# Sixteen-head attention: row maxima passed on per eight heads, and turned scores 17 heads behind the straight ones

## The reference

```python
qkv = x @ in_proj_weight.T + in_proj_bias            # x is the normed input
q, k, v = ...                                        # (B, 16 heads, 256, 8) each
bias = jnp.minimum((pos[:, None] - pos[None, :]) * slopes[:, None, None], MAX_BIAS)
scores = q @ k^T * 8 ** (-0.5) + bias
probs = jax.nn.softmax(scores, axis=-1)
out = (probs @ v) @ out_proj_weight.T + out_proj_bias
```

## Time and profile before

| | us |
|---|---|
| median of 3 runs | 1011.14 (1010.91 to 1011.57) |
| the profiled execution, its own time | 1014.49 |
| its span on the core | 1012.5 |
| mean granted TensorE clock, share of full speed | 0.899 |
| TensorE busy (matmuls) | 795.3 |
| VectorE busy | 550.0 |
| ScalarE busy | 400.2 |
| GpSimd busy | 358.3 |

### The profile page before, as it was taken

One profiled execution on the slowest core, in us unless ns is written; L12 is line 12 of the kernel. 1 busy time (PEld: TensorE's weight loads), 2 busy tenths in 40 slices (PEclk: granted clock), 3 DMA queues, 4 the chain that ended last, 5 costly groups with the idle time before them and its releaser, 6 DMA issues.

```text
span 1012.5 us, 19075 instructions
## 1 busy us (share of the span) xinstructions
PE 795.3 (79%) x5669; PEld 573.7 (57%) x5669; DVE 550.0 (54%) x2190; ACT 400.2 (40%) x945; POOL 358.3 (35%) x543
## 2 busy tenths in 40 slices
PE   0788488999999999932688989889899983029894
PEld 0677365655665777722255666666666652018784
DVE  4677573233222333232777889887897725016772
ACT  0466121222212332200055667665667672015562
POOL 4000517777850232343123323232232011744552
PEclk9999658999999999976579999998999996559998
DMA  9960001111100133114544354433444005111110
GB/s 247 155 207 0 1 1 35 39 42 40 40 0 14 56 110 109 58 52 100 116 93 90 77 106 92 85 86 68 105 90 81 3 3 187 51 56 52 52 50 14
DMA packets 75114, 72.44 MB, mean 72 GB/s; under 512 B 8125, under 2 KB 65680, under 8 KB 72732
## 3 DMA queue, kind: packets, MB, share of 16 engines
q1 hardware_dynamic: 69436, 60.38, 26.6%
q0 software_dynamic: 5600, 11.12, 3.4%
HBM read 43.71 MB, written 27.33 MB: 70 GB/s over the span
## 4 chain that ended last, share of the span: by engine, by line
PE 50%; DVE 14%; issue 10%; DMA 10%; POOL 6%; SPq 4%; ACT 3%; DVEq 2%; POOLq 0%; ACTq 0%
PE bank L1468 10%; PE bank L1469 9%; PE bank L1491 6%; DMA arena<-back_rows 5%; DVE rt L1066 4%; PE bank L1520 4%; POOL sorted_rows L766 3%; PE bank L1610 2%; PE bank L1562 2%; PE bank L1597 2%; PE bank L1592 2%; SPq L527 2%; DMA qk_parts<-arena 2%; SPq L548 1%; PE bank L1411 1%
## 5 line engine op out<-in xcount | busy, mean ns | idle before, releaser
L1066 DVE CUSTOM_DVE_ANT_0 rt<-bank,alibi 128x256 f32<-128x256 f32 x512 | 192.8, 419 | 43.7 <-PE bank L1562 36.6
L1276 ACT ACTIVATE arena<-bank 128x512 f32<-128x512 f32 x256 | 150.6, 597 | 75.7 <-PE bank L1597 69.8
L974 DVE TENSOR_TENSOR arena<-arena,bank 128x512 f32<-128x512 f32 (+1 forms) x128 | 75.1, 587 | 188.6 <-ACT arena L1249 188.6
L1249 ACT ACTIVATE arena<-bank 128x512 f32<-128x512 f32 (+1 forms) x128 | 66.1, 517 | 203.9 <-PE bank L1469 203.9
L1562 PE MATMUL bank<-arena 72*128 72x256 bf16 x512 | 105.9, 292 | 41.0 <-DVE arena L1066 27.1
L1592 PE MATMUL bank<-arena 81*128 81x256 bf16 x512 | 119.3, 279 | 6.5 <-ACT arena L1276 4.6
L1468 PE MATMUL bank<-arena 128*128 128x320 f32 (+2 forms) x256 | 117.2, 540 | 7.3 <-DVE arena L974 7.3
L1469 PE MATMUL bank<-arena 128*128 128x320 f32 (+2 forms) x256 | 112.5, 521 | 0.0
L1562 PEld LDWEIGHTS bank<-arena 72*128 72x128 bf16 x512 | 38.8, 103 | 86.1 <-DVE arena L1066 57.4
L1597 PE MATMUL bank<-arena,ident_b 128*128 128x256 bf16 (+8 forms) x544 | 83.8, 250 | 0.0
L1469 PEld LDWEIGHTS bank<-arena 128*128 128x128 f32 x256 | 49.7, 194 | 43.1 <-issue 32.8
(11 more groups left out here) (236 smaller groups left out, 1378.9 us busy)
## 6 DMA issues: line engine op xcount, KB each, us to landing
arena<-qk_parts SPq DMA_DIRECT2D x48, 192.0 KB
arena<-qk_parts SPq DMA_DIRECT2D x144, 64.0 KB
qk_parts<-arena SPq DMA_DIRECT2D x16, 384.0 KB, 2.8
back_rows<-empty_row SPq DMA_DIRECT2D x1, 4096.0 KB, 38.5
arena<-back_rows SPq DMA_DIRECT2D x16, 256.0 KB, 8.8
arena<-in_w SPq DMA_DIRECT2D x2, 2048.0 KB, 10.9
xg_rows<-empty_row SPq DMA_DIRECT2D x1, 2580.0 KB, 38.5
arena<-xg_rows SPq DMA_DIRECT2D x8, 322.5 KB, 4.0
```

Source lines behind the costliest of these rows:

```text
L974: nc.vector.tensor_tensor(out, sil[:, k, 0:out.shape[1]], bank[4 + k][:, 0:out.shape[1]], ALU.mult).then_inc(hid_done, 1)
L1066: last = nc.vector.tensor_tensor_reduce(biased[n % 2 * QT + u], bank[n % 2][:, SEQ * u:SEQ * u + SEQ], alibi[:, h, P * (1 - u):P * (1 - u) ...
L1249: nc.scalar.activation(sil[:, k, 0:width], bank[2 + k][:, 0:width], ACT.Silu).then_inc(sil_done, 1)
L1276: nc.scalar.activation(prT3[:, n % (2 * HG)].rearrange("p k t -> p (k t)"), bank[2 + n % 2][:], ACT.Exp).then_inc(exp3_done, 1)
```

## The change

- The maxima are handled per half batch m = 0 to 31 of MH = 8 heads: the split at 8m + 9 and 8m + 10, the turning at 8m + 12, the copy at 8m + 13. `max_part` and `max_rest` are half as wide.
- ScalarE issues the DMA of the maxima itself: `copy_max(m)` waits until its own copy is done and issues a DMA of 24 rows into `qs`. `send_max` leaves SP's program. `score_turned` waits for a half's DMA at its first head.
- EXP_LAG goes from 25 to 17, and with it BACK from 45 to 37.
- The steps of the norm move: `combine` from -41 and -40 to -43 and -41, the statistics from -39 to -36, the variance from -38 to -34, `norm3` from -33 to -32. The projection and the copy of q and k stay.
- TURN_5 to LOGITS_5 come two slots earlier behind BACK. ROOT_LAG goes from 5 to 4, so that GpSimd does `root5(c - 4)` behind `parts(c)`.
- The waits on the shared PSUM bank and on the maxima are rewritten for halves.

```diff
-EXP_LAG = 25
-COMBINE_0, COMBINE_1, STATS, VARIANCE, NORM, TURN, HT, QKV, QK_COPY, VALUES = -41, -40, -39, -38, -33, -30, -29, -26, -25, -19
-SPLIT_MAX_0, SPLIT_MAX_1, TURN_MAX, COPY_MAX = NH + 1, NH + 2, NH + 4, NH + 5
+EXP_LAG = 17
+MH = NH // 2
+COMBINE_0, COMBINE_1, STATS, VARIANCE, NORM, TURN, HT, QKV, QK_COPY, VALUES = -43, -41, -36, -34, -32, -30, -29, -26, -25, -19
+SPLIT_MAX_0, SPLIT_MAX_1, TURN_MAX, COPY_MAX = MH + 1, MH + 2, MH + 4, MH + 5
...
-NORM_5, TURN_5, COPY_5, ROUTER_5, LOGITS_5 = BACK + 22, BACK + 27, BACK + 28, BACK + 30, BACK + 31
-ROOT_LAG = 5
+NORM_5, TURN_5, COPY_5, ROUTER_5, LOGITS_5 = BACK + 22, BACK + 25, BACK + 26, BACK + 28, BACK + 29
+ROOT_LAG = 4
...
+def half_batch_at(slot, offset):
+    m, r = divmod(slot - offset, MH)
+    return m if r == 0 and 0 <= m < 2 * BATCH else None
...
-        def send_max(c):
-            wait_apart(sp, (max_rows_done, c + 1))
-            sp.dma_start(qs[MROW:KALL, c % RING], max_rows[0:PARTS * NH, c % 2]).then_inc(max_in[c % 2], 16)
...
-            send_max(c)
...
-        def copy_max(c):
-            act.wait_ge(max_tr, c + 1)
-            if c >= 2:
-                act.wait_ge(max_in[c % 2], 16 * (c // 2))
-            nc.scalar.activation(max_rows[0:PARTS * NH, c % 2], bank[7][0:PARTS * NH, 0:P].bitcast(BF16), ACT.Copy).then_inc(max_rows_done, 1)
+        def copy_max(m):
+            act.wait_ge(max_tr, m + 1)
+            if m >= 2:
+                act.wait_ge(max_in[m % 2], 16 * (m // 2))
+            nc.scalar.activation(max_rows[0:PARTS * MH, m % 2], bank[7][0:PARTS * MH, 0:P].bitcast(BF16), ACT.Copy).then_inc(max_rows_done, 1)
+            c, h = m // 2, MH * (m % 2)
+            wait_apart(act, (max_rows_done, m + 1))
+            act.dma_start(qs[MROW:KALL, c % RING, h:h + MH], max_rows[0:PARTS * MH, m % 2]).then_inc(max_in[m % 2], 16)
...
-            if h == 0:
-                pe.wait_ge(max_in[c % 2], 16 * (c // 2 + 1))
+            if h % MH == 0:
+                m = n // MH
+                pe.wait_ge(max_in[m % 2], 16 * (m // 2 + 1))
```

More of the change, by code:

```diff
@@ L267, in _build @@
     nmax3 = carve([P, 2, QT, NH])
-    max_rest = carve([P, QT, NH])
-    max_part = carve([P, QT, PARTS, NH], BF16)
+    max_rest = carve([P, QT, MH])
+    max_part = carve([P, QT, PARTS, MH], BF16)
     max_rows = carve([P, 2, SEQ], BF16)
@@ L1061, in row_max @@
             wait_apart(dve, (s3_mm, n + 1), *([(max3_done, n - 1)] if n >= 2 else []))
-            if h == 0 and c >= 2:
-                dve.wait_ge(max_parts_done, c - 1)
+            if h % MH == 0 and c >= 2:
+                dve.wait_ge(max_parts_done, n // MH - 3)
             for u in range(QT):
@@ L1069, in row_max, with max_parts_0, max_parts_1 @@
             last.then_inc(max3_done, 1)
-        def max_parts_0(c):
-            wait_apart(dve, (max3_done, NH * (c + 1)), *([(max_tr, c)] if c >= 1 else []))
-            nm = nmax3[:, c % 2]
+        def max_parts_0(m):
+            wait_apart(dve, (max3_done, MH * (m + 1)), *([(max_tr, m)] if m >= 1 else []))
+            nm = nmax3[:, m // 2 % 2, :, MH * (m % 2):MH * (m % 2) + MH]
             nc.vector.tensor_copy(max_part[:, :, 0, :], nm).then_inc(max_split, 1)
-            dve.wait_ge(max_split, 3 * c + 1)
+            dve.wait_ge(max_split, 3 * m + 1)
             nc.vector.tensor_tensor(max_rest, nm, max_part[:, :, 0, :], ALU.subtract).then_inc(max_split, 1)
-        def max_parts_1(c):
-            dve.wait_ge(max_split, 3 * c + 2)
+        def max_parts_1(m):
+            dve.wait_ge(max_split, 3 * m + 2)
             nc.vector.tensor_copy(max_part[:, :, 1, :], max_rest).then_inc(max_split, 1)
-            dve.wait_ge(max_split, 3 * c + 3)
+            dve.wait_ge(max_split, 3 * m + 3)
             nc.vector.tensor_tensor(max_part[:, :, 2, :], max_rest, max_part[:, :, 1, :], ALU.subtract).then_inc(max_parts_done, 1)
@@ L1118, in _ @@
                 row_max(n)
[L1119 to L1122, removed]
+            if (m := half_batch_at(slot3, SPLIT_MAX_0)) is not None:
+                max_parts_0(m)
+            if (m := half_batch_at(slot3, SPLIT_MAX_1)) is not None:
+                max_parts_1(m)
             if (c := batch_at(slot3, COMBINE_0)) is not None:
@@ L1341, in _ @@
                 copy_qk(c)
-            if (c := batch_at(slot3, COPY_MAX)) is not None:
-                copy_max(c)
+            if (m := half_batch_at(slot3, COPY_MAX)) is not None:
+                copy_max(m)
             if (c := batch_at(slot3, COPY_OUT)) is not None:
@@ L1544, in project @@
             if c >= 3:
-                pe.wait_ge(max_rows_done, c - 2)
+                pe.wait_ge(max_rows_done, 2 * c - 4)
             for a in range(2):
@@ L1564, in score, with turn_max @@
             last.then_inc(s3_mm, 1)
[L1566 to L1572, removed]
+        def turn_max(m):
+            pe.wait_ge(max_parts_done, m + 1)
+            if m >= 1:
+                pe.wait_ge(max_rows_done, m)
+            pe.wait_ge(qk3_done, min(m // 2 + 3, BATCH))
+            if m >= 7 and m % 2 == 1:
+                pe.wait_ge(lg5_done, (m - 5) // 2)
             for u in range(QT):
-                last = nc.tensor.transpose(bank[7][0:PARTS * NH, P // 2 * u:P // 2 * u + P // 2].bitcast(BF16),
+                last = nc.tensor.transpose(bank[7][0:PARTS * MH, P // 2 * u:P // 2 * u + P // 2].bitcast(BF16),
                                            max_part[:, u].rearrange("p a h -> p (a h)"), ident_b[:])
@@ L1638, in turn5 @@
             pe.wait_ge(h5_done, e + 1)
-            pe.wait_ge(qk3_done, min(e + 7, BATCH))
-            pe.wait_ge(max_rows_done, min(e + 4, BATCH))
+            pe.wait_ge(qk3_done, min(e + 6, BATCH))
+            pe.wait_ge(max_rows_done, min(2 * e + 7, 2 * BATCH))
             if e >= 1:
@@ L1668, in _ @@
                 project(c)
-            if (c := batch_at(slot3, TURN_MAX)) is not None:
-                turn_max(c)
+            if (m := half_batch_at(slot3, TURN_MAX)) is not None:
+                turn_max(m)
             if (c := batch_at(slot3, TURN_0)) is not None:
```

## The result

The changed kernel takes 1077.4 us (median of 4 runs, 1074.4 to 1080.3) against 1011.0: 6.6% slower, ratio 1.066 (95% interval 1.063 to 1.069). The forecast was 1068, within 1042 to 1100.

A forecast was written before the change was run, and what follows sets the result against it. It took a 41.7 us loop over two batches as the bound, TensorE close behind. Terms -7.5 + 57.2 + 3 + 2.4 + 2 = +57.1 on the profiled 1014.5 gave 1071.6, as a median 1068 us; range 1042 to 1100.

The forecast's parts named there:

- The bound before: Stage of the kernel before: a loop spanning two batches, 41.7 us long, sets the pace, with TensorE close behind.
- the loop of two batches: Copy of q and k, parts, replicate, given-row load, combine, next copy: 41.7 us before, +2.4 us with the change.
- The loop of one batch: Given rows, combine, variance, root5, parts, replicate, next given rows: 27.4 us per batch, +57.2 over nine turns, combines 6 to 15.
- The signs named: Combines 27 us apart, VectorE's given-row wait some 50 us or more, split right behind root5, TensorE idle some 7 us a turn.
- Up to combine 6: Start of the stage: two more slots from combine 4 to the next copies, TensorE slow: +3 us (0 to +6).
- the step on the maxima: Extra VectorE, TensorE and ScalarE work and DMA issues for half batches, covered by TensorE's 8 us idle per turn: 0.
- Behind combine 15: Combine 15 two slots later, +2.4 us; TensorE restarting after an idle stretch, +2 (0 to +5).
- the tail of turned scores: End of the stage: eight slots with turned scores alone go, at 0.94 us each: -7.5 us.
- up to 2.5 us per batch: Cost of the extra small operations and DMA issues for the maxima if no TensorE idle time covered them.
- 8 in all: TensorE's wait per turn if the maxima's DMA landed late: some 4 us twice a batch, equal to its idle time.
- The rival of the cold clock: TensorE drops to 1.2 GHz after idling each turn; if it stays low longer, turns of 31 us, 1100 us; chance 0.09.
- The rival by which the loop of two batches remains: Variance ready in time, so root5 costs parts nothing: +8.7 us, 1020 us; chance 0.12.

The follow-up runs named there:

- Experiment 5: Kernel before the change, with the load of given rows issued ahead of the replicate reads on SP: 995.9 us, ratio 0.982 to the kernel before.
- experiment 7: Kernel before the change, with only the norm's offsets moved as in the change: ratio 1.014 to the kernel before.
- 3: Changed kernel with residual_variance two slots later (BACK + 21 instead of BACK + 19): ratio 1.108 to the kernel before.
- experiment 4: Changed kernel with the load of given rows issued ahead of the replicate reads on SP: ratio 1.001 to the kernel before.
- experiment 1: Changed kernel with residual_variance four slots earlier (BACK + 15 instead of BACK + 19): ratio 1.060 to the kernel before.
- experiment 2: Changed kernel with ROOT_LAG back at 5 instead of 4: ratio 1.116 to the kernel before.
- experiment 8: Changed kernel with the norm's offsets and ROOT_LAG 5 as before, leaving halves, ScalarE's DMA and the lag of 17: ratio 1.137 to the kernel before.

## Why the prediction was right

**The bound before.** Right. Experiment 5 removes the loop of two batches and gains 1.8%, experiment 7 lengthens it by two slots and loses 1.4%.

**The loop of one batch.** Right in place and size: 27.2 us per turn against 27.4, nine turns 244.5 against 246.6. Its two parts fit as well: from the combine to SP's write of the parts 10.0 us against 10.5, from there to the combine it frees 17.2 against 16.9, so a small part of the agreement is two misses that cancel. Each station stands in the chain quoted above; a shift within the loop moves the time (3), and taking the load out of it takes the loss away (4). The signs named came too: VectorE's wait for given rows of 61.4 us, the split right behind `root5`, TensorE idle 5.7 us a turn (I had said some 7).

**Up to combine 6.** The term that was mis-sized: +3 forecast (0 to +6), +11.3 measured. What failed is the step on the maxima, "so 0": it counted ScalarE's DMA as hidden by 8 us of idle time in a turn, and that time exists only once the loop runs, from parts(5) on. Ahead of it a half's DMA met the twelve reads, TensorE waited 5.6 us and came back slow, and the stretch from combine 4 to 5 was 9.2 us longer. The figure of 9.2 us that I gave for a transfer behind a replicate was the right one for this DMA.

**Behind combine 15.** Forecast +2.4 + 2 - 7.5 = -3.1, measured -3.1. The equality is luck: up to the last row maximum it was +3.1 where I had 4.4 (now 881.6 - 809.92, before 812.2 - 743.59), and the tail of turned scores gave -6.2 where I had -7.5 (now 898.8 - 881.6, before 23.4).

**Sum.** Forecast +57.1, measured +64.2 between the profiled spans and +66.3 between the medians. The miss is the first part's.

**What the forecast did not see** is how much it depended on its own idle time. It said what the waits of ScalarE and TensorE would cost without that cover, "up to 2.5 us per batch" and "8 in all", and experiments 1, 2 and 8 gave 6 to 13 us per turn above experiment 4. Over nine turns these are 55, 83 and 116 us more, of which TensorE's busy time, longer by the slow level, is 20, 25 and 70; the rest is idle time, and only in experiment 8 is the clock the larger part. Experiment 1, meant as a cure, failed because a cost that had been covered came out; experiment 2 failed by a step that I had missed, the root ahead of root5. The rival of the cold clock came true in small: each of the nine turns has a clock of 0.87 to 0.94, and the loss fits in TensorE's idle time, as computed. The cause of the changed kernel's time is the load behind the split; the remedy was not to shorten the way to the split but to take the load out from behind it. The rival by which the loop of two batches remains, 1020 us, was never seen by itself: experiment 1, which takes `root5`'s wait out of the way, has the late DMAs of maxima on top.

## What to carry to other kernels

In a pipeline with programs written out per engine, follow each wait back through the queues that it stands in until it closes on itself, and divide the length by the number of batches that it spans. If that is more than the busiest engine's work per batch, it is the turn (27.2 us here, with 19.3 of work on TensorE); if not, the engine is (19.7 with 19.0 of work in experiment 5). A load whose data are ready early doesn't belong behind transfers that wait for late ones; moving one DMA issue was worth 1.8% in the kernel before and 6% in the changed one. And a cost put at nothing because idle time hides it must be priced again before that idle time is taken away.

## What the runs showed of the hardware

- A DMA that ScalarE issues doesn't pass reads that SP has issued. In the changed kernel the 24 packets of 512 bytes of a half's DMA issued at 542.09, with no reads in flight, start 1.4 us after the issue, and it lands after 2.0. In the case above the first of them starts 7.0 us after the issue and the DMA lands after 9.2; up to its first packet only packets of SP's queue run, of 8192 and 1024 bytes. In experiment 1, right behind the reads, it lands after up to 11.3. This is no sooner than the load of given rows in SP's own queue, mostly 8 to 11 us. By the Trainium skill ("DMA: Bandwidth & Descriptors", Queues, rings and completion order) each DMA engine alternates between the rings of different issuers; if it did so between these two, the small DMA should have been done early in the drain. The measurement decides: a separate queue gave no precedence here. The same page says (Issuing engines are not separate DMA queues) that issuing from several engines saves issue time only, and these runs agree in that the DMA did not land sooner.
- Issuing 24 rows and 48 rows cost ScalarE the same 0.74 us, and 0.96 us of its time with the wait for its copy. Sending a batch in two halves doubled what its DMAs cost the engine.
- TensorE's granted clock fell with its stops, between the levels of 2.4 and 1.2 GHz. Over nine turns it was 1.00 in experiments 4 and 5, whose stops are 1.2 us at most; 0.92 in the changed kernel, with one stop of 3.1 to 6.2 us in each turn; and 0.70 in experiment 8, with one stop of 2.1 to 4.9 us and one of 1.6 in each turn. At 0.70 practically the same matmuls took 27.1 us instead of 19.4. The length of one stop alone doesn't tell: behind a stop of 1.7 us at 596.0 in the kernel before the clock stayed at 1.00, behind one of 1.6 us at 708.4 in experiment 8 it was 0.57 over the next 11 us.
